# A two-layer decoder kernel: cross keys and values among the self scores, the cross norm with gamma and residual in two operations, the first pairs earlier, the performer reordered

## The chip, the cores and the metric

The kernel runs on one core of a Trainium2 chip. The metric is device microseconds (us) of one execution. The engines are TensorE (PE; its weight loads are PEld), VectorE (DVE), ScalarE (ACT), GpSimd (POOL) and SyncE (SP), which issues the transfers. Each runs its own list of instructions in order, and they wait for each other on semaphores.

## The reference

Six layers on x of 4 batches x 512 tokens x 256 channels, each followed by a residual and a layer norm:

```python
x = _layernorm(x + _L0_attn_ref(x, Wk, Wq, Wv))                      # causal softmax attention, 1 head
x = _layernorm(x + _L0_xattn_ref(x, ctx, ctx, mask, ...))            # cross attention, ends in:
    #   normed = (context - mu) * rsqrt(var + EPS);  return normed * ln_gamma + ln_beta
x = _layernorm(x + _L0_ffn_ref(x, k0, k1, k2, s0, s1, s2))           # three layers with weights +1 / -1
x = _layernorm(x + _L1_attn_ref(x, Wqkv, bqkv, Wout, bout, proj))    # performer, 16 heads of 16:
    #   q' = relu(q proj), k' = relu(k proj), 64 features a head, causal:
    #   out = sum_{s<=t} (q'_t . k'_s) v_s / (sum_{s<=t} q'_t . k'_s + 1e-6)
x = _layernorm(x + _L1_xattn_ref(x, ctx, ctx, ...))                  # mLSTM, 8 heads of 32, gates from x and ctx
x = _layernorm(x + _L1_ffn_ref(x, w1, conv_w, conv_b, w2))           # quantized layer, convolution, SiLU, quantized layer
```

## The kernel before

**Stages.** The work of a batch is cut in two. The front half has self attention (`self.`), cross attention (`cross.`), the sign layers (`sign.a`, `b`, `c`) and the performer (`perf.`). The back half has the mLSTM (`mlstm.`) and the quantized layers (`quant.`). The front half of batch b+1 is issued among the back half of batch b, so the program is: one front half alone, with the preparation of weights (`prep.`) in it, three middle stages with both, and one back half alone.

**Order.** Nothing is scheduled at run time. Each engine has a generator for each half, which yields a step's name (`cross.score0`) ahead of the step's instructions. `weave` takes from the generators in the order of a rank per step and engine, read from tables (`FRONT_TIMES`, `BACK_TIMES`, `PREP_TIMES`: name, then the ranks for PE, DVE, ACT, POOL), with `PERIOD` between batches and `LATER` between the halves. The order within a half's generator never changes by the ranks; how the two halves lie in each other does.

**Banks.** TensorE writes to 8 PSUM banks, 4 for each half, taken in rotation as the plan (`fb.use`, `bb.use`) lists them. A step that fills a bank waits until the bank's last user emptied it.

**Attention.** Scores of token tile i, the transposes ("turn") of tile i-1 and the products with the values of tile i-2 follow each other, i = 0 to 5. VectorE takes row maxima, ScalarE the exponential. The keys and values of the cross attention come from the context (`ctxT`) alone, so they depend on nothing that the self attention makes.

**Norms.** `stats` (DVE: statistics, aggregate, +eps), `rstd` (POOL: power), `normalize` (DVE: `shift`, tile 2p; ACT: tile 2p+1). Tiles go in pairs p = 0, 1; then TensorE turns a pair to channels (`xT0`, `xT1`), and DVE or ACT copy the result out of the bank. In the cross attention, the norm of the context is followed by DVE's product with gamma (L1434) and the residual (L1438), each of 256 columns per tile, and then by the statistics of the layer's own norm.

**Sign layers.** `sign.a` multiplies 8 column blocks m over 2 x 2 accumulated parts. The first four m are done for the first pair alone, while the second is still in its norm: L919 in the trace, then L928 for what is left, L938 for layer b, L948 for c.

**Performer.** Two chunks c of 8 heads. Projections: v (L803), q and k (L795); features of q and k (L974), keys' features turned (L983), the state (L1000) and its sums (L1530, L1532 on DVE); scores of two heads at a time (L1018), masked by DVE and ACT; then, for each group of four heads, the denominators (L1028) and the numerators (L1041), whose matmuls write to 32 rows of a bank with a column group of the array each:

```python
for i in range(2):
    for j in (2 * g, 2 * g + 1):
        ins = nc.tensor.matmul(num.bank[32 * j:32 * j + 32, here], ...
                               tile_position=(0, 32 * j), skip_group_check=True)
```

GpSimd sets `v_pad` and `p_sums` to zero in every batch, and copies the values into `v_pad`. Both lie in a region that other steps use too.

## Time and profile before

| | |
|---|---|
| three runs | 1008.03, 1002.79, 1007.87 us, median 1007.87 |
| profiled execution | 1005.53 us, of which the span from first to last instruction 1004.3 |
| mean granted TensorE clock | 0.867 of full |
| busy: PE / DVE / ACT / POOL | 805.1 / 622.3 / 357.8 / 169.6 us |
| DMA | 25 GB/s over the span |

Busy times are sums over the span; what a change is worth depends on which engine's work ends last at its place. The span splits into 0 to 207 us (front half alone), 207 to 429, 429 to 651, 651 to 873 (middle stages) and 873 to 1004 (back half alone). In the timeline rows a bracket behind a group of instructions gives the engine's idle time before it and who released it; a group's mean duration overlaps with its neighbours, because matmuls are pipelined. "L803" is line 803 of the kernel before. In the changed kernel the same lines stand 14 to 50 lines further down.

### The profile page before, as it was taken

Reading aid. Unit: us, or ns where it says so; the run is one execution under the profiler, and the core shown is the slowest. Engines: PE = TensorE matmul, PEld = TensorE weight load, DVE = VectorE, ACT = ScalarE, POOL = GpSimd, SP = SyncE. Lnnn points to the kernel's source line nnn. Section 1 sums busy time; section 2 is a strip of 40 time slices with the busy share of each in tenths; the row PEclk is TensorE's granted clock in tenths of the full one; section 3 lists DMA queues with packets and bytes.
Section 4 is the critical chain, followed back from the end, with each engine's and each line's share of the span. In section 5 each row is a group of like instructions: output and inputs, shape, how many; then the busy total and the mean of one; then the engine's idle time right before and its main releaser. Section 6 shows DMA issues by size and latency. Waiting matters only on the chain.

```text
span 1004.3 us, 14662 instructions
## 1 busy us (share of the span) xinstructions
PE 805.1 (80%) x5789; PEld 566.0 (56%) x5832; DVE 622.3 (62%) x1535; ACT 357.8 (36%) x646; POOL 169.6 (17%) x250
## 2 busy tenths in 40 slices
PE   8859877788999877888999877898999877739124
PEld 5545546666774545756774655766764555628112
DVE  2867322247487666656586767556685768455786
ACT  3242111125532254235432345244432445143062
POOL 3210110012322110012322300013312300003300
PEclk9989978699879979899979979998979978967565
DMA  9210000010010000020010000010000000000000
GB/s 367 104 43 1 1 21 1 1 64 22 1 43 1 1 22 1 1 85 22 1 43 1 1 22 2 1 64 1 24 19 1 1 1 1 23 0 1 0 0 21
DMA packets 13507, 25.85 MB, mean 26 GB/s; under 512 B 768, under 2 KB 7040, under 8 KB 13184
## 3 DMA queue, kind: packets, MB, share of 16 engines
q1 hardware_dynamic: 13440, 24.92, 7.2%
q8 instruction: 46, 0.75, 0.3%
q14 instruction: 21, 0.17, 0.1%
HBM read 22.82 MB, written 2.10 MB: 25 GB/s over the span
## 4 chain that ended last, share of the span: by engine, by line
PE 61%; DVE 24%; issue 7%; ACT 6%; POOL 2%; DVEq 0%; POOLq 0%; ACTq 0%
PE bank L938 11%; PE bank L795 7%; PE bank L803 6%; PE bank L1018 4%; PE bank L843 3%; PE bank L826 2%; PE bank L974 2%; PE bank L1041 2%; PE bank L948 2%; PE bank L928 2%; DVE stats L1289 2%; PE bank L788 1%; DVE work L1816 1%; DVE work L1785 1%; PE bank L1250 1%
## 5 line engine op out<-in xcount | busy, mean ns | idle before, releaser
L2110 POOL TENSOR_TENSOR rstd<-rstd,minus_half 128x2 f32<-128x2 f32 x56 | 40.3, 719 | 510.1 <-DVE rstd L1295 510.1
L938 PE MATMUL bank<-work,f0w 128*128 128x512 f16 x512 | 111.2, 379 | 0.0
L938 PEld LDWEIGHTS bank<-work,f0w 128*128 128x128 f16 x512 | 50.1, 98 | 60.4
L1959 ACT ACTIVATE work<-bank 128x512 f16<-128x512 f32 x64 | 37.3, 597 | 95.3 <-PE bank L938 76.5
L1477 DVE SCALAR_TENSOR_TENSOR work<-bank,work 128x512 f16<-128x512 f32 x64 | 41.7, 685 | 29.9 <-ACT work L1959 29.9
L1018 PE MATMUL bank<-work 64*128 64x128 f32 x512 | 44.5, 323 | 15.0 <-DVE work L1532 11.0
L1552 DVE TENSOR_TENSOR work<-bank,upper 128x512 f32<-128x512 f32 x32 | 22.1, 690 | 50.7 <-PE bank L1018 50.7
L1992 ACT ACTIVATE work<-bank 128x512 f32<-128x512 f32 x32 | 19.0, 592 | 90.1 <-PE bank L1018 90.1
L843 PE MATMUL bank<-work 128*128 128x256 f32 x208 | 50.6, 389 | 0.0
L1639 DVE TENSOR_TENSOR work<-work 128x512 f32<-128x512 f32 x32 | 25.7, 830 | 38.3 <-ACT work L2036 38.0
L1000 PE MATMUL bank<-work 128*128 128x34 f32 x192 | 35.5, 360 | 10.1 <-DVE work L1518 10.1
L1018 PEld LDWEIGHTS bank<-work 64*128 64x128 f32 x512 | 37.6, 222 | 9.5 <-issue 9.5
L843 PEld LDWEIGHTS bank<-work 128*128 128x128 f32 x208 | 39.1, 196 | 4.7
L1000 PEld LDWEIGHTS bank<-work 128*128 128x128 f32 x192 | 34.6, 281 | 11.6 <-ACT work L1978 11.6
L1197 PEld LDWEIGHTS bank<-work 128*128 128x128 f32 x256 | 39.3, 242 | 1.0 <-issue 1.0
L1373 DVE TENSOR_REDUCE small<-bank 128x1 f32<-128x512 f32 (+3 forms) x32 | 18.8, 587 | 33.7 <-PE bank L827 28.1
L1197 PE MATMUL bank<-work 128*128 128x33 f32 x256 | 39.0, 315 | 0.8 <-DVE work L1639 0.8
L1289 DVE BATCH_NORM_STATS2 stats<-y 128x6 f32<-128x256 f32 x96 | 36.1, 414 | 5.8 <-ACT y L1938 5.7
L974 PE MATMUL bank<-work,perf_w 32*128 32x512 f32 x128 | 23.0, 790 | 20.0 <-ACT work L1982 14.9
L2185 POOL TENSOR_TENSOR small<-small,minus_half 128x8 f32<-128x8 f32 x16 | 27.2, 1702 | 64.5 <-DVE small L1700 64.5
L2150 POOL COPY work<-work 128x256 f32<-128x256 f32 x16 | 10.2, 667 | 149.4 <-PE bank L1041 147.7
L1876 ACT ACTIVATE work<-bank,small 128x512 f32<-128x512 f32 (+3 forms) x32 | 19.4, 606 | 42.9 <-DVE small L1373 42.8
(271 smaller groups left out, 1860.8 us busy)
## 6 DMA issues: line engine op xcount, KB each, us to landing
ctxT<-in_ctxT SPq DMA_DIRECT2D x8, 512.0 KB, 4.7
work<-in_mask SPq DMA_DIRECT2D x4, 1024.0 KB, 5.9
xT<-in_xT SPq DMA_DIRECT2D x4, 512.0 KB, 3.6
work<-in_w SPq DMA_DIRECT2D x1, 2048.0 KB, 18.6
ctx<-in_ctx SPq DMA_DIRECT2D x4, 512.0 KB, 3.8
out<-y SPq DMA_DIRECT2D x4, 512.0 KB, 3.0
perf_w<-in_perf_w SPq DMA_DIRECT2D x1, 1536.0 KB, 16.3
x<-in_x SPq DMA_DIRECT2D x2, 512.0 KB, 6.3
```

Of the source, the lines that this page charges most:

```text
L795: ins = nc.tensor.matmul(u.bank[:, :], weights[:, k, c0:c0 + P], src[:, k, :], start=(k == 0), stop=(k == NC - 1))
L803: ins = nc.tensor.matmul(u.bank[:, j * C:(j + 1) * C], src[:, k, t * P:(t + 1) * P], weights[:, k, c0:c0 + C], start=(k == 0), stop=(k == ...
L843: ins = nc.tensor.matmul(u.bank[:, 0:C], probT[:, t % 2, j * P:(j + 1) * P], v[:, j, :], start=(j == 0), stop=(j == n - 1))
L938: ins = nc.tensor.matmul(u.bank[:, :], f0w1[:, k, m * P:(m + 1) * P], h1[part][:, k, :], start=(k == 0 and part == 0), stop=(k == NF - 1 a ...
L974: nc.tensor.matmul(u.bank[:, :], proj[rows, c, j * P:(j + 1) * P], src[rows, c, :], start=True, stop=True, tile_position=(32 * j, 0)).then ...
L1000: ins = nc.tensor.matmul(u.bank[:, o:o + 2 * PV1], kfs[:, t - 1, j * P:(j + 1) * P], p_v1[:, t - 1, h:h + 2, :].rearrange("p a b -> p (a b ...
L1018: ins = nc.tensor.matmul(u.bank[:, here], kf[rows, j, here], qf[rows, j, here], start=(i == 0), stop=True, tile_position=(PM * i, 0), skip ...
L1197: ins = nc.tensor.matmul(u.bank[:, h * LV1:(h + 1) * LV1], cT[:, h, t * P:(t + 1) * P], l_v1[:, t, h, :], start=True, stop=True)
L1289: m = vec.mark(nc.vector.bn_stats(s.stats[:, t, :], src[:, t, :]))
L1477: low_part(what, m, dst, number + m, lambda o, x, hi: nc.vector.scalar_tensor_tensor(out=o, in0=x, scalar=0.0, in1=hi, op0=ALU.max, op1=AL ...
L1959: nc.scalar.activation(dst[0][:, m, :], u.bank[:, :], ACT.Relu).then_inc(high_made.sem, 1)
L2110: nc.gpsimd.tensor_tensor(s.rstd[:, two], s.rstd[:, two], minus_half[:, 0:2], ALU.pow).then_inc(s.rstd_made.sem, 1)
```

## The change

Six things, in the order of the diff.

- All rank tables, `PERIOD` and `LATER` are changed.
- The four projections for the cross keys and values are issued among the self attention's steps, one behind each of the first four (`AMONG`), with a buffer of its own for the values (`c_v`).
- The cross norm: right behind its statistics, (y - mean) * gamma in one DVE operation per tile; then, when GpSimd's power is there, times rstd plus x in a second. ScalarE has no part in it any more.
- The first pair of the sign layers is evicted ahead of the norm of the second pair on both engines; three column blocks (before: four) are then multiplied for the first pair alone, ahead of `sign.xT1`.
- The performer: on ScalarE the copy of `xT0` ahead of the second norm; on TensorE xT0, v0, xT1, q and k of chunk 0, v1, features of q, q of chunk 1, features of k, k of chunk 1. Heads are taken in the order `taken`, so that every group of four has its numerators in four column groups. `v_pad` and `p_sums` are buffers of their own, set to zero once.
- x is loaded behind the context and the cross weights.

```diff
+AMONG = ("ck0", "ck1", "cv0", "cv1")
...
-PERIOD, LATER = 4120, 50
+PERIOD, LATER = 4780, 25
...
+    v_pad = sb("v_pad", [P, NT, HALF, 2, PD])
+    p_sums = sb("p_sums", [P, NT - 1, PAIRS, 32])
...
+    taken = [0, 3, 4, 7, 2, 1, 6, 5]
...
                 if 1 <= i <= NT:
                     turn_t(i - 1)
+                if i < len(among):
+                    yield f"{name}.{AMONG[i]}"
+                    among[i]()
                 if i >= 2:
...
+            yield from attention("self", b, front.xT, a_v, lambda t: bar_later[:, :], True,
+                                 [lambda: second_keys(0), lambda: second_keys(1),
+                                  lambda: second_values(0), lambda: second_values(1)])
...
+            yield "sign.xT0"
+            wait_normed(front, b, 2, 0)
+            to_channels(fb["sign", b, "xT", 0], fx[b % 2], 0)
+            yield "sign.early"
...
+            for m in range(3):
...
+            yield "sign.xT1"
...
-                for m2 in range(4) if m == 0 else ():
...
+                    if c == 0:
+
+                        yield f"perf.{made}.1"
+                        project_T(fb["perf", b, 1, made], wqkvT, {"q": 0, "k": C}[made] + P, front.xT)
...
-                        for i in range(2):
-                            for j in (2 * g, 2 * g + 1):
-                                ins = nc.tensor.matmul(num.bank[32 * j:32 * j + 32, here],
-                                                       v_pad[:, t, 2 * j + i, :, :].rearrange("p a b -> p (a b)"),
-                                                       inner[:, (2 * j + i) % 4, here], start=False, stop=(i == 1),
-                                                       tile_position=(0, 32 * j), skip_group_check=True)
+                        for r in range(4 * g, 4 * g + 4):
+                            h, j = taken[r], taken[r] // 2
+                            ins = nc.tensor.matmul(num.bank[32 * j:32 * j + 32, here],
+                                                   v_pad[:, t, h, :, :].rearrange("p a b -> p (a b)"),
+                                                   inner[:, r % 4, here], start=False, stop=(g == 1),
+                                                   tile_position=(0, 32 * j), skip_group_check=True)
...
+            def spread_by_gamma(p):
+
+                yield f"cross.in_norm{p}"
+                for t in (2 * p, 2 * p + 1):
+                    spread[t] = vec.mark(nc.vector.scalar_tensor_tensor(
+                        out=front.y[:, t, :], in0=front.y[:, t, :], scalar=front.mv[:, t, 0:1], in1=gamma,
+                        op0=ALU.subtract, op1=ALU.mult))
+
             def add_residual(p):
                 yield f"cross.add{p}"
-                dve.wait_ge(*front.normed_v.at(b, front.place[1, p]))
-                dve.wait_ge(*front.normed_s.at(b, front.place[1, p]))
-                for t in (2 * p, 2 * p + 1):
-                    m = vec.mark(nc.vector.tensor_tensor(front.y[:, t, :], front.y[:, t, :], gamma, ALU.mult))
-                dve.wait_ge(*m)
+                dve.wait_ge(*front.rstd_made.at(b, front.place[1, p]))
+                dve.wait_ge(*spread[2 * p + 1])
                 dve.wait_ge(*front.shifted.at(b, NT - 1))
                 for t in (2 * p, 2 * p + 1):
-                    added[t] = vec.mark(nc.vector.tensor_tensor(front.y[:, t, :], front.y[:, t, :], fx[b % 2][:, t, :],
-                                                                ALU.add))
...
+                    added[t] = vec.mark(nc.vector.scalar_tensor_tensor(
+                        out=front.y[:, t, :], in0=front.y[:, t, :], scalar=front.rstd[:, t:t + 1], in1=fx[b % 2][:, t, :],
+                        op0=ALU.mult, op1=ALU.add))
...
+        nc.gpsimd.memset(v_pad[:, :, :, :, :], 0.0).then_inc(constants_by_gpsimd, 1)
+        nc.gpsimd.memset(p_sums[:, :, :, :], 0.0).then_inc(constants_by_gpsimd, 1)
...
-            pool.wait_ge(*v1_ones.at(b))
-            nc.gpsimd.memset(v_pad, 0.0)
-            nc.gpsimd.memset(p_sums, 0.0).then_inc(blocks_zeroed.sem, 1)
-            pool.wait_ge(*blocks_zeroed.at(b))
```

How the tables and the code together move instructions shows in the order of each engine.

TensorE at the start of the performer in a middle stage, before: `ident,x` are the pairs turned, `perf_w` the projections and the features (L974), `work,f1w` the quantized layer and `identb,work` the turns of the back half.

```order
L788 MATMUL bank<-ident,x 128x128 x4
L1204 MATMUL bank<-ident,small 128x128 x4
L803 MATMUL bank<-perf_w,xT 128x256 x4
L788 MATMUL bank<-ident,x 128x128 x4
L1216 MATMUL bank<-identb,work 128x128 x4
L795 MATMUL bank<-work,f1w 128x512 x12
L803 MATMUL bank<-perf_w,xT 128x256 x4
L795 MATMUL bank<-xT,perf_w 128x512 x8
L974 MATMUL bank<-work,perf_w 128x512 x8
L795 MATMUL bank<-work,f1w 128x512 x4
L983 MATMUL bank<-perf_w,work 128x128 x12
L1000 MATMUL bank<-work 128x34 x12
```

And with the change (L1002 are the features; L809 with `xT,perf_w` x2 are q and k of one chunk):

```order
L802 MATMUL bank<-ident,x_other 128x128 x4
L809 MATMUL bank<-xT,perf_w 128x512 x4
L817 MATMUL bank<-perf_w,xT 128x256 x4
L1002 MATMUL bank<-work,perf_w 128x512 x4
L809 MATMUL bank<-xT,perf_w 128x512 x2
L1002 MATMUL bank<-work,perf_w 128x512 x4
L809 MATMUL bank<-xT,perf_w 128x512 x2
L1015 MATMUL bank<-perf_w,work 128x128 x12
L809 MATMUL bank<-work,f1w 128x512 x4
L1032 MATMUL bank<-work 128x34 x12
L809 MATMUL bank<-work,f1w 128x512 x2
L1044 MATMUL bank<-bar_upper,identb 128x512
```

The values of the first pair stand ahead of the turning of the second, chunk 1's q and k between and behind the features, and six matmuls of the back half next to the state (L1032, before L1000).

VectorE in the first front half, between the last row maximum of the cross attention and its residual, before (L1434 and L1438 are gamma and residual):

```order
L1289 BN_STATS stats<-y 128x6 x2
L1292 BN_AGGR mv<-stats 128x2 x2
L1295 TENSOR_SCALAR rstd<-mv 128x2
L1377 RECIPROCAL small<-small 128x1
L1301 SCALAR_TENSOR_TENSOR shift<-mv,rstd 128x2
L1304 TENSOR_SCALAR y<-y,mv,rstd 128x256
L1434 TENSOR_TENSOR y<-y,rows_all 128x256 x2
L1438 TENSOR_TENSOR y<-y,x 128x256 x2
L1289 BN_STATS stats<-y 128x6 x2
```

And with the change (L1467 is the spread by gamma; L1364 and L1366 turn a block of weight bits to +1 and -1, and six such pairs stand ahead of these rows, behind L1467):

```order
L1364 TENSOR_SCALAR f0w<-ctxT 128x1024
L1366 TENSOR_SCALAR f0w<-f0w,s_cols 128x1024
L1369 TENSOR_SCALAR f0w<-y 128x512 x4
L1477 SCALAR_TENSOR_TENSOR y<-y,rstd,x 128x256 x2
L1321 BN_STATS stats<-y 128x6 x2
L1324 BN_AGGR mv<-stats 128x2 x2
L1327 TENSOR_SCALAR rstd<-mv 128x2
L1321 BN_STATS stats<-y 128x6 x2
L1324 BN_AGGR mv<-stats 128x2 x2
```

The preparation of the sign weights, which stood among the steps of the self attention, stands between spread and residual (L1477).

TensorE at the cross attention in a middle stage, before: L1122 are the back half's gate scores, `ident,x` and L895 the turned pairs and their queries, L826 and L827 the cross scores, L1138 to L1150 the columns of the mLSTM's gates.

```order
L834 MATMUL bank<-ident,work 128x128 x4
L843 MATMUL bank<-work 128x256 x7
L795 MATMUL bank<-ctxT,cross_w 128x512 x4
L803 MATMUL bank<-cross_w,ctxT 128x256 x8
L1122 MATMUL bank<-xT,ctxT 128x128 x16
L788 MATMUL bank<-ident,x 128x128 x4
L895 MATMUL bank<-xT,cross_w 128x256 x4
L788 MATMUL bank<-ident,x 128x128 x4
L895 MATMUL bank<-xT,cross_w 128x256 x4
L826 MATMUL bank<-work 128x512 x2
L827 MATMUL bank<-work,identb 128x512
L1138 MATMUL bank<-small,ones 128x72
```

And with the change (L1154 are the gate scores, L802 and L915 the pairs and queries, L840 the scores, L848 and L857 turns and products):

```order
L848 MATMUL bank<-ident,work 128x128 x4
L857 MATMUL bank<-work 128x256 x7
L1154 MATMUL bank<-xT,ctxT 128x128 x32
L802 MATMUL bank<-ident,x 128x128 x4
L915 MATMUL bank<-xT,cross_w 128x256 x4
L802 MATMUL bank<-ident,x 128x128 x4
L915 MATMUL bank<-xT,cross_w 128x256 x4
L840 MATMUL bank<-work 128x512 x2
L841 MATMUL bank<-work,identb 128x512
L840 MATMUL bank<-work 128x512 x2
L841 MATMUL bank<-work,identb 128x512
L848 MATMUL bank<-ident,work 128x128 x4
```

Both lots of gate scores stand together, the projections of keys and values (L795, L803 with `cross_w`) have gone ahead among the self scores, and the columns stand behind the cross attention's products.

## Rows read from the trace of the kernel before

**Rows 1.** The page's part 4: the chain of waits by engine and by line.

```profile
PE 61%; DVE 24%; issue 7%; ACT 6%; POOL 2%; DVEq 0%; POOLq 0%; ACTq 0%
PE bank L938 11%; PE bank L795 7%; PE bank L803 6%; PE bank L1018 4%; PE bank L843 3%; PE bank L826 2%; PE bank L974 2%; PE bank L1041 2%; PE bank L948 2%; PE bank L928 2%; DVE stats L1289 2%; PE bank L788 1%; DVE work L1816 1%; DVE work L1785 1%; PE bank L1250 1%
```

**Rows 2.** Windows by stage: window, its length, busy us (instructions) by engine, granted clock, DMA.

```profile
429.00:651.00 222.00, 193.55 (x1445) 137.00 (x1455) 148.10 (x366) 87.44 (x157) 40.71 (x58) 0.92 0.06 20
585.00:601.00 16.00, 13.05 (x123) 9.96 (x117) 12.79 (x26) 8.39 (x14) 0.00 (x0) 0.61 0.01 2
118.00:158.00 40.00, 29.08 (x161) 19.94 (x162) 10.96 (x27) 6.82 (x13) 5.87 (x10) 0.70 0.05 14
```

**Rows 3.** Timeline of PE: one lot of denominators (L1028) and of numerators (L1041).

```profile
603.49 0.64 PE L1028 MATMUL bank<-work,head_col 128*32 128x128 f32 x16 [0.20 <-DVE work L1552]
603.95 1.92 PE L1041 MATMUL bank<-work 128*32 128x128 f32 x32
```

**Rows 4.** Groups by line and shape, weight loads, 429 to 651 us.

```profile
L1041 PEld LDWEIGHTS bank<-work 128*32 128x32 f32 x128 | 7.0, 110 | 0.0
L1028 PEld LDWEIGHTS bank<-work,head_col 128*32 128x32 f32 x128 | 3.0, 109 | 3.0 <-DVE work L1552 2.5
```

**Rows 5.** Timeline of PE, performer in a middle stage.

```profile
565.59 1.99 PE L803 MATMUL bank<-perf_w,xT 128*128 128x256 f32 x8 [1.74 <-ACT xT L1850]
...
581.29 1.14 PE L974 MATMUL bank<-work,perf_w 32*128 32x512 f32 x8 [0.94 <-DVE work L1507]
584.25 2.09 PE L974 MATMUL bank<-work,perf_w 32*128 32x512 f32 x8 [1.81 <-ACT work L1982]
...
590.22 4.48 PE L1000 MATMUL bank<-work 128*128 128x34 f32 x24 [1.34 <-DVE work L1518]
595.98 2.08 PE L1018 MATMUL bank<-work 64*128 64x128 f32 x16 [1.28 <-DVE work L1532]
...
623.61 3.81 PE L1000 MATMUL bank<-work 128*128 128x34 f32 x24 [1.20 <-DVE work L1518]
```

**Rows 6.** Timeline of PE: the performer's state in the first front half.

```profile
147.67 5.30 PE L1000 MATMUL bank<-work 128*128 128x34 f32 x24 [1.31 <-DVE work L1518]
```

**Rows 7.** Timeline of PE, cross attention to second sign layer (L938), middle stage.

```profile
468.62 1.97 PE L895 MATMUL bank<-xT,cross_w 128*128 128x256 f32 x8 [0.87 <-DVE xT L1281]
470.42 1.88 PE L826 MATMUL bank<-work 128*128 128x512 f32 x4
474.24 0.41 PE L1138 MATMUL bank<-small,ones 8*128 8x72 f32 x2 [1.94 <-DVE small L1632]
...
526.16 4.05 PE L938 MATMUL bank<-work,f0w 128*128 128x512 f16 x18
```

**Rows 8.** Groups by line and shape, ACT, 429 to 651 us: copies of gate scores.

```profile
L2013 ACT ACTIVATE work<-bank 128x512 f32<-128x512 f32 x8 | 4.1, 597 | 0.0
```

**Rows 9.** Timeline of PE, first front half: pairs turned for the sign layers.

```profile
67.82 0.63 PE L788 MATMUL bank<-ident,x 128*128 128x128 f32 x4 [4.00 <-DVE x L1304]
...
73.12 1.08 PE L788 MATMUL bank<-ident,x 128*128 128x128 f32 x4 [4.56 <-ACT x L1857]
```

**Rows 10.** Groups by line, DVE, 28 to 60 us: preparing the sign weights.

```profile
L1334 DVE TENSOR_SCALAR f0w<-f0w,s_cols 128x1024 f16<-128x1024 f16 x8 | 4.2, 530 | 0.3
L1332 DVE TENSOR_SCALAR f0w<-xT 128x1024 f16<-128x1024 uint8 x4 | 3.8, 947 | 0.0
L1332 DVE TENSOR_SCALAR f0w<-ctxT 128x1024 f16<-128x1024 uint8 x4 | 2.7, 686 | 0.0
```

**Rows 11.** The chain of waits, first front half, cross norm: start, us, what.

```profile
67.97 0.61 ACT y L1857
...
68.67 0.77 DVE y L1434 x2
```

**Rows 12.** Timeline of DVE around the last front half's end.

```profile
872.29 0.74 DVE L1289 BATCH_NORM_STATS2 stats<-y 128x6 f32<-128x256 f32 x2
...
878.83 0.16 DVE L1301 SCALAR_TENSOR_TENSOR shift<-mv,rstd 128x2 f32<-128x2 f32 x1 [0.81 <-POOL rstd L2110]
```

787 lines of the change are left out of this document (402 added, 385 removed).

## The prediction

> **What bounds the kernel now.** First the chain of waits, which says whose work sets the end: TensorE 61% of it, VectorE 24%, and no transfer among the leading lines [rows 1]. The program is a pipeline: the front half of batch b+1 runs beside the back half of batch b. The windows by stage show one middle stage of 222.0 us with TensorE busy for 193.55, VectorE for 148.10, at a granted clock of 0.92 [rows 2]. Three such stages (207 to 873), the first front half alone (0 to 207) and the last back half alone (873 to 1004) make the span of 1004.3 us. So time comes out of a middle stage in three ways: TensorE's 28 us without work, work that it does at a low clock, and work that gets shorter. Then the timeline of TensorE, read where the gaps are. They lie where one tensor is handed from engine to engine: in the start of the performer [rows 5], in the cross attention and the norm behind it [rows 7], and, in the first front half, where no back half fills them, in both [rows 6, 9]. Behind such gaps the clock is low: 0.61 from 585 to 601, 0.70 from 118 to 158 [rows 2].
>
> The sum is made against the profiled execution: 1005.53 us, that is the span and 1.2 us around it. The median of the runs is 2.3 us above it.
>
> **The change, part by part.**
>
> Performer numerators. 32 matmuls fall in every group of four heads: two groups, two chunks, four batches, so 16 such lots, all on the chain (L1041 is 2% of it [rows 1]). Now neighbours use two column groups in turn and take 1.92 us. The denominators beside them, 16 matmuls of the same shape over four column groups, take 0.64 us [rows 3]. The reordered heads put four column groups into each lot, so 32 should take 2 x 0.64 = 1.28: 0.64 less by these rows, 0.45 less against the 1.73 us that the lot holds the chain. I take 0.56, times 16: **-9 us**. Bounds: nothing, if it is the loading of a new weight for every matmul that sets the pace (128 loads keep the loader busy for 7.0 us here, for 3.0 in the denominators, at the same 110 and 109 ns each [rows 4]); or half of 1.92, -15.
> The Trainium skill ("TensorEngine Tiling (Array Packing)", Key Properties) says that tiles work independently and load and multiply in parallel; four groups for two would then halve the lot, -15 us by the rule against -9 by the row. No row here shows these loads over four groups.
>
> Performer start, middle stages. The same matmuls are ordered anew, so what counts is the gaps [rows 5]. At 565.59 TensorE waited 1.74 us for ScalarE's copy of xT; that copy now stands ahead of the second norm on ScalarE: about 0.6 less. At 581.29, 0.94 for the eviction of the last keys; now values stand between: gone. At 584.25, 1.81 for the first features; now q of chunk 1, four matmuls of 512 columns, stands between: gone. At 590.22, 1.34, and at 595.98, 1.28, on VectorE; lots of 4 and 2 matmuls of the back half's quantized layer now stand there, which stood elsewhere: 0.9 and 0.4 less. Sum 4.65. I take **-4 us** a stage, three times -12: a little is lost because the chain's VectorE work (with SiLU and convolution work of the back half between) does not get shorter. Bounds: 0, if VectorE is what is late and the gaps only move to the state; -7.5, if with the gaps the low clock goes too (the state at 590.22 takes 4.48 us, at 623.61, at a higher clock, 3.81).
>
> Performer start, first front half. The same gaps, with no back half to fill them, and all the work of 124 to 158 at half clock: the state takes 5.30 us [rows 6] for 3.81, and the features 2.09 for 1.14, as at 584.25 and 581.29 [rows 5]. The two gaps that fall, as long as those at 581.29 and 584.25, give 2.7; the clock, if it stays up, another 5 to 6 over the stretch. I take **-7 us**, bounds -3 and -10.
>
> Cross attention in the middle stages. Keys and values now stand among the self scores. TensorE had work there anyway, so nothing is removed. What moves: the back half's gate scores (L1122, 2 x 16 matmuls, one lot each side of the projections) now stand next to each other. The second lot needs banks that ScalarE has to empty, four copies of 0.597 us [rows 8]: a wait of some 2 us. On VectorE the gate's sum g, its row maximum and the negative of it now stand ahead of the copy of the second xT, some 2 us more in all: the query projection, 0.87 late today [rows 7], is 2 to 3 late. So the first cross score comes some 4 us later than at 470.42 [rows 7]. Behind it the reverse: the columns' matmuls at 474.24 waited 1.94 us for VectorE's columns, now they come after the four cross score lots. The norm with gamma loses a ScalarE pass and VectorE's gamma products (0.61 and 0.77 us [rows 11]) and the shift ahead of them; the product by gamma now lies beside GpSimd's power. Each of two chains is 1.5 to 1.7 us shorter. And the first pairs are turned before the second norm, so that early matmuls cover its latency. From first score to the second sign layer it is 55.7 us today [rows 7]; I estimate 50.7. Net **-1 us** a stage, -3 in all, and either sign is open: bounds -5 and +13 (below).
>
> First front half, cross norm. VectorE's preparation of the sign weights was spread over 30 to 55 us, beside TensorE's self attention. Now seven pairs of operations, three of 0.95 + 0.53 us and four of 0.69 + 0.53 [rows 10], and four small ones, an estimated 9.9 to 10.7 us together, stand in one lump between the spread by gamma and the residual. TensorE has only the last cross products beside it. The pairs that it waits for at 67.82 and 73.12 [rows 9] would come at about 73 and 77; the shorter norm gives 1.7 twice, the early matmuls some more. I take **+3 us**, bounds 0 and +7.
>
> Last stage. The evictions of the performer's output on VectorE stood behind one norm of the back half: its statistics start at 872.29 [rows 12]. That norm is 0.74 for the statistics, some 0.4 for their aggregation, 0.81 of waiting for GpSimd [rows 12] and some 0.6 for shift and scale: 2.5 us. Now two norms and a residual product of some 0.5 stand ahead, 5.6 us. Less the slack at the second projection, **+2.5 us** where nothing covers it; in a middle stage front work of the next batch does, +0.5, which is inside the -4 and -1. Bounds 0 and +3.5.
>
> The zeroing of two buffers once instead of per batch is on GpSimd, behind the constants at the start, and saves work later on an engine that is busy for 41 of 222 us [rows 2]: nothing. The changed order of the loads: nothing, no transfer stands on the chain [rows 1]; if the later load of x is late, it is by less than one load, and only once.
>
> Sum: -9 - 12 - 7 - 3 + 3 + 2.5 = -25.5, 1005.5 - 25.5 = **980 us**.
>
> **The rivals.**
> *It goes nowhere.* VectorE and GpSimd chains, not TensorE's order, are late: the performer's gain (-19) is only -6, the numerators give -4, the cross attention loses 2 a stage, the lump 6. Then -6 - 4 + 6 + 6 + 2.5: 1005 to 1008. For it: the waits at 590.22 and 595.98 name VectorE [rows 5]. Against: those at 565.59 and 584.25 name ScalarE, which is free. 0.11.
> *Slower.* The place is TensorE ahead of the first cross score. Two waits of 2 to 3 us each, close together, are what is seen ahead of low clocks: a gap of 4.00 and one of 4.56 at 67.82 and 73.12 [rows 9], the short gaps of rows 5 ahead of 0.61. If the clock falls there, the cross attention (an estimated 12 to 13 us at full speed: four lots of scores of 1.88 [rows 7], products and turns of two thirds of that) takes twice as long: with the waits, +13 a stage less what the norm gives back, some +10; three times 30, less the 25.5 + 3 of the rest: +2 at least, and with the lump at its bound and little from the performer +12, so 1007 to 1018. It decides from 9 us a stage. Against: today's gaps of 0.87 and 1.94 [rows 7] lie in the same place, and the stage still has a clock of 0.92. 0.15.
> *The numerators don't speed up*, all else as forecast: 985 to 995. The equal load times of rows 4 speak for it, the row of denominators, which also load each time, against. 0.12.
> *More.* The clock stays up in all performer starts and in the norm: middle stages at -12: 957 to 965. 0.10.
>
> **How the numbers follow.** The forecast (966 to 994) has 0.52. Slower and nowhere together have 0.26, so the range ends at 1007, where about 0.12 is left above; below 957 some 0.08 is left. What a measurement of this kernel can tell from no change is about 0.5%, 5 us. Faster: 0.52 + 0.12 + 0.10 = 0.74; same 0.11; slower 0.15.
>
> **What would show it.** In the changed kernel's timeline: numerator lots of 1.2 to 1.4 us; performer start without waits on the features, first performer scores 4 us earlier against the end of the sign layers (8 in the first front half), and a clock above 0.8 where it was 0.61; a lump of VectorE preparation beside an idle TensorE near 65 to 75 us; middle stages of 214 to 216 us. A wait of over 2 us ahead of the first cross score, with half clock behind it, would make the prediction wrong towards slower; numerator lots still at 1.9 would take 9 us from it.

## The result, and the profile after

The changed kernel takes 976.79 us in the median of four runs (971.01 to 992.32), the kernel before 1005.33 (1002.71 to 1008.03) beside it: the ratio is 0.970, 95% interval 0.961 to 0.978. The forecast was 980, in a range of 957 to 1007. Ratios leave out runs more than 1.5% above the fastest of their kernel; medians are over all runs.

The changed kernel spreads over 20 us, the kernel before over 5. Six more runs of it (experiment c1 below) had their median at 984.96; over all ten it is 982. Where experiments are compared with it, a difference of medians under some 8 us therefore says little by itself, and the stretches of one profiled execution decide. Its own profiled execution took 971.75 us, near its fast end.

The page of the changed kernel, parts 1, 2 and 4: busy time, granted clock in 40 slices, and the chain. Its span is 970.5 us.

```profile
PE 771.9 (80%) x5816; PEld 524.1 (54%) x5816; DVE 615.4 (63%) x1519; ACT 354.0 (36%) x638; POOL 165.3 (17%) x244
...
PEclk9978998798899999899899998999899997857565
...
PE 63%; DVE 26%; ACT 5%; issue 4%; POOL 1%; DVEq 0%; ACTq 0%
```

TensorE is busy for 33.2 us less, and the span is 33.8 us shorter; its share of the chain is 63%, 61% before [rows 1]. The mean granted clock rises from 0.867 to 0.899. TensorE's time without work is the same over the whole span, 199.2 us before and 198.6 after: what fell is its busy time. Windows of a middle stage, of the performer's start in it, and of the performer's start in the first front half, which answer to [rows 2]:

```profile
412.00:624.00 212.00, 183.63 (x1452) 125.25 (x1453) 146.97 (x363) 86.55 (x155) 39.67 (x56) 0.97 0.07 21
554.00:570.00 16.00, 11.25 (x74) 5.71 (x73) 9.61 (x15) 9.42 (x18) 1.83 (x3) 1.00 0.11 34
118.00:150.00 32.00, 24.31 (x154) 15.31 (x153) 12.45 (x35) 6.69 (x12) 5.13 (x9) 0.94 0.06 17
```

TensorE's time without work in the stage has hardly moved: 28.4 us now, 28.45 before. What fell is its busy time, by 9.9 us, and with it the low clock: 0.61 has become 1.00, and 0.70 has become 0.94.

The table shows where the 33.8 us lie, read from the starts of matmuls on TensorE. A stage runs from the start of the performer's output product in one batch to that of the next; the last column is the back half alone.

| us | first front half | middle 1 | middle 2 | middle 3 | last back half |
|---|---|---|---|---|---|
| before | 206.7 | 222.0 | 221.9 | 221.9 | 131.9 |
| changed | 198.0 | 213.8 | 211.6 | 213.6 | 133.5 |
| difference | -8.7 | -8.2 | -10.3 | -8.3 | +1.6 |

The second middle stage by stretch. The last column adds up TensorE's waits in the stretch (the brackets of its timeline), before and after:

| us | before | changed | difference | forecast | waits |
|---|---|---|---|---|---|
| output product to first cross score | 41.7 | 44.0 | +2.3 | +4 | 3.7, 6.0 |
| first cross score to second sign layer (L938, now L961) | 55.7 | 48.6 | -7.2 | -5 | 4.1, 1.6 |
| second sign layer to third | 27.6 | 27.6 | 0 | 0 | 0, 0 |
| third sign layer to first performer score | 42.2 | 40.5 | -1.7 | -4 | 9.3, 9.1 |
| first performer score to output product | 54.6 | 51.0 | -3.6 | -2.2 (4 lots) | 11.0, 11.7 |

PE's timeline, one lot of denominators and numerators, and the weight loads of the same lines over the stage, for [rows 3, 4]:

```profile
578.75 0.64 PE L1060 MATMUL bank<-work,head_col 128*32 128x128 f32 x16 [0.20 <-DVE work L1602]
579.22 1.06 PE L1073 MATMUL bank<-work,v_pad 128*32 128x128 f32 x32
...
612.44 1.08 PE L1060 MATMUL bank<-work,head_col 128*32 128x128 f32 x32
```

```profile
L1073 PEld LDWEIGHTS bank<-work,v_pad 128*32 128x32 f32 x128 | 3.6, 110 | 0.0
L1060 PEld LDWEIGHTS bank<-work,head_col 128*32 128x32 f32 x128 | 3.1, 109 | 2.0 <-DVE work L1602 1.4 <-issue 0.2
```

A lot takes 1.06 us where it took 1.92. One load still takes 110 ns, but the loader is busy for 3.6 us instead of 7.0. The 128 loads add up to 14.1 us, so in the mean two lay over each other before and four do now: loads of different column groups overlap. Over the whole span the loader's time for these lots falls from 28.1 to 14.3 us and the matmuls' from 30.7 to 16.9, by the same 13.8.

PE's timeline at the performer's start in a middle stage, for [rows 5], and the first two waits and the state in the first front half, for [rows 6]:

```profile
541.84 1.99 PE L817 MATMUL bank<-perf_w,xT 128*128 128x256 f32 x8 [0.67 <-ACT xT L1900]
...
556.84 1.14 PE L1002 MATMUL bank<-work,perf_w 32*128 32x512 f32 x8 [1.33 <-DVE work L1540]
558.62 1.98 PE L809 MATMUL bank<-xT,perf_w 128*128 128x512 f32 x4 [0.64 <-ACT work L2035]
561.47 1.14 PE L1002 MATMUL bank<-work,perf_w 32*128 32x512 f32 x8 [0.87 <-ACT work L2018]
563.25 1.98 PE L809 MATMUL bank<-xT,perf_w 128*128 128x512 f32 x4 [0.64 <-ACT work L2035]
566.17 0.95 PE L1015 MATMUL bank<-perf_w,work 32*128 32x128 f32 x24 [0.94 <-DVE work L1548]
...
568.43 2.84 PE L1032 MATMUL bank<-work 128*128 128x34 f32 x24 [0.34 <-DVE work L1566]
...
572.16 0.39 PE L1044 MATMUL bank<-bar_upper,identb 128*128 128x512 bf16 x1 [0.46 <-DVE work L1583]
```

```profile
122.35 1.97 PE L817 MATMUL bank<-perf_w,xT 128*128 128x256 f32 x8 [0.72 <-issue]
...
143.79 2.88 PE L1032 MATMUL bank<-work 128*128 128x34 f32 x24 [1.30 <-DVE work L1566]
```

The waits are not gone. They are cut into pieces of 0.34 to 1.33 us, with matmuls of some 2 us between, and from the third sign layer to the first score they add up to 9.1 us, 9.3 before. In the first front half they do shrink, from 10.9 to 7.7 us, 2.6 of it at the copy of `xT0` (0.72 for 3.33). The state now takes 2.84 us where it took 4.48 and 5.30: it does the same work at the full clock.

PE's timeline at the cross attention of a middle stage, for [rows 7]:

```profile
447.92 1.17 PE L1154 MATMUL bank<-xT,ctxT 32*128 32x128 f32 x32 [2.23 <-ACT work L2069]
...
450.35 1.99 PE L915 MATMUL bank<-xT,cross_w 128*128 128x256 f32 x8 [0.68 <-ACT xT L1900]
...
454.04 1.97 PE L915 MATMUL bank<-xT,cross_w 128*128 128x256 f32 x8 [1.25 <-DVE xT L1313]
455.84 1.88 PE L840 MATMUL bank<-work 128*128 128x512 f32 x4
...
504.40 1.89 PE L961 MATMUL bank<-work,f0w 128*128 128x512 f16 x8
```

The wait of 2.23 us on ScalarE's copies of gate scores stands where the forecast put one of some 2, and the query projection is 1.25 late. In this stage and the third no low clock follows. In the first middle stage one does, behind the same wait of 2.23 us: the granted clock is 0.51 from 235 to 242 us, and the query projection takes twice as long:

```profile
236.94 3.78 PE L915 MATMUL bank<-xT,cross_w 128*128 128x256 f32 x8 [0.68 <-ACT xT L1900]
```

There the first cross score comes 4.5 us later than before, not 2.3. Behind the first score, to the second sign layer, it is 48.56 us, 55.74 before, in all three middle stages. 2.6 us of that are waits; most of the rest is the clock ahead of the second sign layer, 0.53 from 509 to 520 before, 1.00 from 486 to 505 now.

The first front half, DVE's lump (its first pair and the residual behind it; six more pairs like the first and four small operations lie between) and PE beside it, for [rows 9, 10]:

```profile
58.38 0.68 DVE L1364 TENSOR_SCALAR f0w<-xT 128x1024 f16<-128x1024 uint8 x1
59.09 0.48 DVE L1366 TENSOR_SCALAR f0w<-f0w,s_cols 128x1024 f16<-128x1024 f16 x1
...
67.58 0.87 DVE L1477 SCALAR_TENSOR_TENSOR y<-y,rstd,x 128x256 f32<-128x256 f32 x2
```

```profile
62.08 3.78 PE L857 MATMUL bank<-work 128*128 128x256 f32 x8 [3.76 <-ACT work L1948]
72.32 1.09 PE L802 MATMUL bank<-ident,x 128*128 128x128 f32 x4 [6.46 <-DVE x L1336]
```

The wait of 3.76 us is not VectorE's. ScalarE sums the sizes of the quantized layer's weights (L1917) from 56.56 to 61.47 us, 4.9 us in one piece, and the copy that TensorE waits for (L1948) stands behind it.

The last place is the end of the last front half, where the quantized layer's norm releases the pair for the mLSTM:

```profile
837.01 3.72 PE L817 MATMUL bank<-perf_w,y 128*128 128x256 f32 x16 [1.40 <-DVE y L1616]
846.93 1.09 PE L802 MATMUL bank<-ident,x 128*128 128x128 f32 x4 [6.20 <-ACT x L1907]
```

### The profile page after: what moved, and what is told of

It is laid out like the page before. It is cut to its first block, busy times and chain, and to the rows that moved or that the text cites. A ratio compares the mean times of both kernels' runs of the same rounds, so it can differ in the third digit from the quotient of the medians.

```text
span 970.5 us, 14621 instructions
## 1 busy us (share of the span) xinstructions
PE 771.9 (80%) x5816; PEld 524.1 (54%) x5816; DVE 615.4 (63%) x1519; ACT 354.0 (36%) x638; POOL 165.3 (17%) x244
## 4 chain that ended last, share of the span: by engine, by line
PE 63%; DVE 26%; ACT 5%; issue 4%; POOL 1%; DVEq 0%; ACTq 0%
PE bank L961 11%; PE bank L809 5%; PE bank L817 5%; PE bank L840 4%; PE bank L857 3%; PE bank L1050 3%; PE bank L1229 2%; PE bank L951 2%; PE bank L1032 2%; DVE work L1819 2%; PE bank L1002 2%; PE bank L971 2%; DVE work L1825 2%; PE bank L802 2%; DVE work L1828 1%
## 5 line engine op out<-in xcount | busy, mean ns | idle before, releaser
L961 PE MATMUL bank<-work,f0w 128*128 128x512 f16 x512 | 111.3, 379 | 0.0
L961 PEld LDWEIGHTS bank<-work,f0w 128*128 128x128 f16 x512 | 50.1, 98 | 60.2
L857 PE MATMUL bank<-work 128*128 128x256 f32 x208 | 51.6, 391 | 3.8 <-ACT work L1948 3.8
L1405 DVE TENSOR_REDUCE small<-bank 128x1 f32<-128x512 f32 (+3 forms) x32 | 18.9, 590 | 54.6 <-PE bank L841 54.5
L1689 DVE TENSOR_TENSOR work<-work 128x512 f32<-128x512 f32 x32 | 27.3, 860 | 27.4 <-ACT work L2092 27.2
L857 PEld LDWEIGHTS bank<-work 128*128 128x128 f32 x208 | 39.0, 195 | 9.1 <-ACT work L1948 4.2
L1050 PE MATMUL bank<-work 64*128 64x128 f32 x512 | 41.8, 309 | 0.0
L1050 PEld LDWEIGHTS bank<-work 64*128 64x128 f32 x512 | 35.1, 209 | 8.6 <-issue 8.6
L809 PE MATMUL bank<-xT,perf_w 128*128 128x512 f32 x64 | 30.7, 612 | 8.2 <-ACT work L2035 5.1
L1229 PE MATMUL bank<-work 128*128 128x33 f32 x256 | 33.4, 288 | 0.8 <-DVE work L1689 0.8
L1229 PEld LDWEIGHTS bank<-work 128*128 128x128 f32 x256 | 33.2, 209 | 1.5 <-issue 1.5
L1032 PE MATMUL bank<-work 128*128 128x34 f32 x192 | 28.2, 313 | 7.1 <-DVE work L1566 7.1
L1570 DVE TENSOR_SCALAR work<-bank 128x512 f32<-128x512 f32 x24 | 15.8, 688 | 27.5 <-PE bank L1002 27.1
L1032 PEld LDWEIGHTS bank<-work 128*128 128x128 f32 x192 | 27.4, 230 | 9.4 <-ACT work L2031 9.4
```

Source lines behind the costliest of these rows:

```text
L809: ins = nc.tensor.matmul(u.bank[:, :], weights[:, k, c0:c0 + P], src[:, k, :], start=(k == 0), stop=(k == NC - 1))
L857: ins = nc.tensor.matmul(u.bank[:, 0:C], probT[:, t % 2, j * P:(j + 1) * P], v[:, j, :], start=(j == 0), stop=(j == n - 1))
L961: ins = nc.tensor.matmul(u.bank[:, :], f0w1[:, k, m * P:(m + 1) * P], h1[part][:, k, :], start=(k == 0 and part == 0), stop=(k == NF - 1 a ...
L1032: ins = nc.tensor.matmul(u.bank[:, o:o + 2 * PV1], kfs[:, t - 1, j * P:(j + 1) * P], p_v1[:, t - 1, h:h + 2, :].rearrange("p a b -> p (a b ...
L1050: ins = nc.tensor.matmul(u.bank[:, here], kf[rows, pair, here], qf[rows, pair, here], start=(i == 0), stop=True, tile_position=(PM * i, 0) ...
L1229: ins = nc.tensor.matmul(u.bank[:, h * LV1:(h + 1) * LV1], cT[:, h, t * P:(t + 1) * P], l_v1[:, t, h, :], start=True, stop=True)
```

## The experiments

Twelve kernels ran: ten with one edit to the changed kernel, one without an edit (c1), and one that joins two (d1). Each figure is a median with its range and number of runs, then the ratio to the kernel before on the same chip.

**a1, two column groups again.** The heads in their natural order, the matmuls of a lot alternating between two groups. All else stays changed.

```diff
-    taken = [0, 3, 4, 7, 2, 1, 6, 5]
+    taken = list(range(8))
...
-                        for r in range(4 * g, 4 * g + 4):
+                        for r in (4 * g, 4 * g + 2, 4 * g + 1, 4 * g + 3):
...
-                                                   inner[:, r % 4, here], start=False, stop=(g == 1),
+                                                   inner[:, r % 4, here], start=False, stop=(h % 2 == 1),
```

> The changed kernel with the heads in their natural order and the numerators' matmuls taking two column groups in turn, as before the change; all else as changed. Theory (the lots of numerators got shorter because neighbouring matmuls now stand in four column groups): each of the 16 lots goes back from 1.06 us to about 1.92, the performer's second part of every stage grows by 4 x 0.86 = 3.4 us, and the whole by 13 to 14 us against 971.8, so about 985. Rival (the shorter lots come from the new buffer of the padded values or from a clock that is higher there): lots stay near 1.1 us and the time within 3 us of the changed kernel.

Measured: 993.87 us (987.62 to 1002.39, 4), ratio 0.9895 (0.983 to 0.996). Its lot:

```profile
156.10 1.92 PE L1073 MATMUL bank<-work,v_pad 128*32 128x128 f32 x32
```

The lot is back at 1.92. 16 x 0.86 = 13.8 us of the difference to the changed kernel are the lots, which TensorE shows as 30.7 us busy against 16.9 over 512 matmuls. The rest, 3 us by medians, is inside the spread. `v_pad` is a buffer of its own here too, so the new buffer does not shorten the lots.

**b5, two groups, in pairs one behind the other.** Does the taking turns matter, or the number of groups?

```diff
-    taken = [0, 3, 4, 7, 2, 1, 6, 5]
+    taken = list(range(8))
...
-                                                   inner[:, r % 4, here], start=False, stop=(g == 1),
+                                                   inner[:, r % 4, here], start=False, stop=(h % 2 == 1),
```

> The changed kernel with the heads in their natural order and the numerators' matmuls in that order too, so that two neighbours stand in one column group before the next follows (groups 0 0 1 1). Theory (a matmul in a column group waits for the one ahead of it in the same group, and different groups run beside each other): the lot of 32 takes longer than the 1.92 us of groups in turn, 2.5 us or more, and the kernel is 5 us or more slower than with two groups in turn (987.6 at the least). Rival (only how many groups a lot touches counts): 1.92 us again.

Measured: 991.39 us (989.61 to 995.98, 4), ratio 0.988 (0.985 to 0.991).

```profile
590.34 1.94 PE L1073 MATMUL bank<-work,v_pad 128*32 128x128 f32 x32
```

Groups 0 0 1 1 take 1.94 us, groups 0 1 0 1 take 1.92, four groups 1.06. The number of groups in a lot counts; the order of two groups does not.

**a2, the copy behind the norm.** In the first batch ScalarE copies `xT0` behind the second norm, as before.

```diff
-            yield "perf.xT0"
-            copy_pair(fb["perf", b, "xT", 0], front.xT, 0)
+            if b > 0:
+                yield "perf.xT0"
+                copy_pair(fb["perf", b, "xT", 0], front.xT, 0)
             yield from normalize(front, b, 3, front.y, fx[b % 2], 1, "sign.")
+            if b == 0:
+                copy_pair(fb["perf", b, "xT", 0], front.xT, 0)
```

> The changed kernel with ScalarE's copy of the performer's first turned pair behind the second pair's norm again, in the first front half alone. Theory (this copy was the 3.33 us gap ahead of the first values, and the gap was what lowered the clock behind it): the gap ahead of the first values grows from 0.72 to about 3.3 us, and the performer's first part runs at half clock: from the last sign layer to the first performer score 6 to 9 us more, the whole 6 to 9 us more, about 979. Rival (the clock is set by the many short gaps behind, not by this one): only the 2.6 us of the gap, about 974 to 975.

Measured: 982.86 us (979.63 to 993.06, 4), ratio 0.981 (0.974 to 0.988).

```profile
124.81 2.85 PE L817 MATMUL bank<-perf_w,xT 128*128 128x256 f32 x8 [3.33 <-issue]
```

The gap of 3.33 us is back for 0.72, and the projection behind it takes 2.85 for 1.97. From the third sign layer to the first performer score the first front half takes 37.8 us instead of 34.0, 2.5 of it waits, and as a whole 201.4 instead of 198.0. So this copy is 3.8 of the 9 us that the performer's start gained there. The low clock of the whole stretch did not come back with it: the state takes 3.07 us.

**a3, chunk 1's q and k ahead of the features.** The order of before on TensorE and on the engines that evict; nothing else.

```diff
             yield from values(1)
+            for made in "qk":
+                yield f"perf.{made}.1"
+                project_T(fb["perf", b, 1, made], wqkvT, {"q": 0, "k": C}[made] + P, front.xT)
             for c in range(NC):
...
-                    if c == 0:
-
-                        yield f"perf.{made}.1"
-                        project_T(fb["perf", b, 1, made], wqkvT, {"q": 0, "k": C}[made] + P, front.xT)
...
```

> The changed kernel with the queries and keys of chunk 1 projected ahead of the features again, in all batches. Theory of the prediction (they cover TensorE's waits at the features): 2 to 3 us more in each of four performer starts, 8 to 12 us in all, 980 to 984. Theory from the trace after the change (with four banks in rotation every lot waits for an eviction of the lot before, 0.64 and 0.87 us, wherever the projections stand, so the waits were only cut up): between -2 and +3 us in all, 970 to 975.

Measured: 989.98 us (989.24 to 997.49, 4), ratio 0.987 (0.982 to 0.991). The lot of projections now lies in one piece, and the old waits behind it are back:

```profile
353.80 1.14 PE L1003 MATMUL bank<-work,perf_w 32*128 32x512 f32 x8 [0.93 <-DVE work L1545]
356.76 1.14 PE L1003 MATMUL bank<-work,perf_w 32*128 32x512 f32 x8 [1.81 <-ACT work L2033]
359.37 0.95 PE L1012 MATMUL bank<-perf_w,work 32*128 32x128 f32 x24 [1.47 <-DVE work L1569]
```

From values to first score the middle stages take 30.2, 34.3 and 31.7 us, against 30.7, 30.7 and 30.6. In the first of them the order alone costs nothing. In the second and third the same instructions take 3.6 and 1.0 us longer. TensorE's waits from the third sign layer to the first score are 8.2 to 8.6 us here and 9.1 in the changed kernel, so the reordering removes no waiting. In the middle stages it keeps the clock up. All four runs have a mean clock of 0.866 to 0.870, as low as before the change, where the changed kernel's ten have 0.879 to 0.903. And the state, which comes right behind, takes 3.00, 5.17 and 3.24 us in this kernel's middle stages, 4.48 or 4.49 in the kernel before, and 2.84 to 2.95 in all thirty middle stages of the ten profiled executions that have the new order and no filling matmuls. What that is worth is not shown: none of the four runs came under 989 us, but other stretches, which the edit leaves alone, were longer in this execution too.

**a4, the preparation spread.** The ranks of the weight preparation go back among the steps of the self and cross attention, VectorE's and also ScalarE's sums of sizes (`prep.abs`).

```diff
-    ("prep.w00", None, 445, None, None),
+    ("prep.w00", None, 230, None, None),
...
-    ("prep.w11", None, 520, None, None),
-    ("prep.w12", None, 520, None, None),
+    ("prep.w11", None, 380, None, None),
+    ("prep.w12", None, 424, None, None),
...
-    ("prep.abs00", None, None, 516, None),
+    ("prep.abs00", None, None, 370, None),
...
```

> The changed kernel with the preparation of the sign weights on VectorE and of the sums of sizes on ScalarE put into the gaps of the self and cross attention of the first front half; three of the twelve VectorE steps stay between the spread by gamma and the residual. Theory (the lump of 9.2 us on VectorE between 58.4 and 67.6, and 4.9 us on ScalarE from 56.6 to 61.4, make the first pair late): the first pair is turned at 65 to 67 instead of 72.3, the second sign layer begins 5 to 7 us earlier, the whole falls by 4 to 7 us, to 965 to 968. Rival (the gap of 3.76 us before the last product and the norm's own chain hold it): less than 2 us earlier.

Measured: 969.29 us (968.88 to 976.98, 4), ratio 0.966 (0.962 to 0.971).

```profile
55.34 3.62 PE L857 MATMUL bank<-work 128*128 128x256 f32 x16
65.63 1.09 PE L802 MATMUL bank<-ident,x 128*128 128x128 f32 x4 [6.67 <-DVE x L1336]
```

The gap of 3.76 us inside the products is gone, the one ahead of the pair is not: it is the latency of two norms. From first cross score to the first sign matmul it is 27.2 us instead of 33.4. The two lumps, VectorE's and ScalarE's, cost 6.2 us there; they were not spread one at a time. The first front half as a whole is only 1.6 us shorter, 196.5 against 198.0: the next stretch takes 1.2 more, and from the third sign layer to the first performer score, and from there to the output product, it is 2.3 and 1.6 more, with the same instructions and the same waits (7.7 and 11.6 us), so by the clock.

**b1, keys and values behind the self attention.**

```diff
-        plan_attention("self", b, [("cross", b, "k", 0), ("cross", b, "k", 1), ("cross", b, "v", 0), ("cross", b, "v", 1)])
+        plan_attention("self", b)
...
-    ("self.cv0", 147, 180, None, None),
+    ("self.cv0", 147, 216, None, None),
...
```

> The changed kernel with the cross keys' and values' projections behind the self attention again, on all engines; all else as changed. Theory (TensorE had work there anyway; in the first front half the stretch from the self queries to the first cross score is 32.4 us in both kernels): 0 to 1.5 us a stage, the time within 5 us of the changed kernel's 971 to 977. Rival (they fill the softmax's waits in the self attention, which the changed rank tables count on): 3 us or more in every stage, 984 and up.

Measured: 1006.99 us (998.83 to 1037.75, 10), ratio 1.000 (0.997 to 1.004): the whole gain is gone. The profiled execution was the longest of the ten, so its lengths are not used, only what waits:

```profile
465.90 1.09 PE L851 MATMUL bank<-ident,work 128*128 128x128 f32 x4 [3.53 <-ACT work L1931]
...
481.42 1.17 PE L1159 MATMUL bank<-xT,ctxT 32*128 32x128 f32 x32 [2.23 <-ACT work L2074]
```

With the projections away, the last turns of the self attention wait 3.53 us for ScalarE's exponential. The wait on the gate scores is the same 2.23. So in the changed kernel, with its rank tables, the projections among the scores fill waits. They are not what the change gained: the kernel before has them behind too, and its waits from the output product to the first cross score are 3.7 us a stage, where they are 9.4 here and 5.6 to 6.0 in the changed kernel. The loss is not the clock alone either: two runs with a mean clock of 0.890 take 999.34 and 998.83 us, two of the changed kernel with 0.891 take 981.83 and 982.08. The other half's steps lie otherwise in the changed tables, and the projections belong to them.

**b2, the gate scores apart.** The second lot behind the queries, by its rank.

```diff
-    ("mlstm.raw1", 238, None, 397, None),
+    ("mlstm.raw1", 275, None, 397, None),
```

> The changed kernel with the second lot of the back half's gate scores moved on TensorE from ahead of the cross attention's pairs to behind its first score, by one rank. Theory (the wait of 2.23 us that the prediction foresaw, for ScalarE's four copies, is a loss): it goes, the first cross score of each middle stage comes 3.3 us earlier and the first sign layer 2 us earlier; 3 x 2.2 = 6 to 7 us less in all, 964 to 970. Rival (the pair's norm on VectorE, which the copy of the second turned pair waits behind, holds the queries anyway): the wait moves to the pairs, less than 2 us in all.

Measured: 988.34 us (986.09 to 1003.64, 4), ratio 0.983 (0.979 to 0.987).

```profile
664.74 1.17 PE L1154 MATMUL bank<-xT,ctxT 32*128 32x128 f32 x32
668.58 0.63 PE L802 MATMUL bank<-ident,x_other 128*128 128x128 f32 x4 [2.66 <-issue]
```

The 2.23 us are not saved. They stand ahead of the turned pair now, 2.66 us. The releaser is not named, but ScalarE's list shows it: the four copies of gate scores (2.06 us from 665.93) stand ahead of its tile of the pair's norm (0.62 us from 667.86), so TensorE waits for ScalarE's copies in both kernels, only at another step. Another order on ScalarE was not tried.

**b3, gamma behind the power.** VectorE waits for GpSimd's power before it multiplies by gamma.

```diff
                 yield f"cross.in_norm{p}"
+                dve.wait_ge(*front.rstd_made.at(b, front.place[1, p]))
```

> The changed kernel with the product by gamma made to wait for GpSimd's power, so that it no longer lies beside it. Theory (the overlap is part of the chain's gain): 0.8 us for each of two pairs in the first front half, where nothing covers it, and 0 to 0.8 for the second pair in a middle stage: 1.5 to 4 us in all. Rival (VectorE has other work in that time anyway, preparation in the first front half and the mLSTM's later): nothing, within 1 us in the stages' lengths.

Measured: 998.83 us (990.39 to 1005.56, 10), ratio 0.993 (0.990 to 0.996). VectorE and GpSimd in the middle stage:

```profile
488.16 0.17 DVE L1327 TENSOR_SCALAR rstd<-mv 128x2 f32<-128x2 f32 x1
496.95 0.88 DVE L1468 SCALAR_TENSOR_TENSOR y<-y,mv,rows_all 128x256 f32<-128x256 f32 x2 [8.62 <-POOL rstd L2169]
```

```profile
490.04 3.48 POOL L2227 TENSOR_TENSOR work<-ctx,small 128x256 f32<-128x256 f32 x6 [13.43 <-ACT small L2086]
493.49 2.77 POOL L2173 TENSOR_TENSOR x<-x,rows_all 128x256 f32<-128x256 f32 x4
496.21 0.71 POOL L2169 TENSOR_TENSOR rstd<-rstd,minus_half 128x2 f32<-128x2 f32 x1
```

The power was asked for at 488.3 and made at 496.9: ten operations of the back half stand ahead of it in GpSimd's list. In the changed kernel the same queue lets the power start at 480.02, 10 us after VectorE's request at 469.96, but the product with gamma does not hang on it. In the kernel before, GpSimd had been idle for 12.85 us when the power was asked for. So the product beside the power is worth more than the 0.81 us of [rows 12]: with it behind, VectorE stands still for 8.62 us, and the back half's work in its list with it. The stretch from score to first sign matmul is 38.7 to 39.2 us in the middle stages for 36.9, and 35.3 for 33.4 in the first. Those 1.8 to 2.4 us at four places make 8 of the 27 us by which the profiled execution is longer than the changed kernel's (the medians are 22 apart, where 4 at most were expected). Most of the rest lies in stretches that the edit leaves alone.

**b4, the last norms spread.** Performer evictions on VectorE between the quantized layer's two norms, by rank.

```diff
-    ("perf.spread.1", 1886, 1522, 1812, None),
+    ("perf.spread.1", 1886, 1560, 1812, None),
...
-    ("quant.norm0", None, 1592, 1925, None),
+    ("quant.norm0", None, 1520, 1925, None),
```

> The changed kernel with the last layer's two norms on VectorE moved ahead of and between the performer's last masks, away from the place ahead of the performer's output. Theory (the two norms and a residual product ahead of the copies cost 2.5 us where the last back half stands alone, and 0.5 in the middle stages): the last stage falls by 2 to 3 us, the others by 0 to 1: 968 for 971. Rival (they then delay the masks, for which TensorE waits): the last performer part grows by as much.

Measured: 993.44 us (990.63 to 996.74, 4), ratio 0.988 (0.984 to 0.993).

```profile
856.05 5.41 PE L817 MATMUL bank<-perf_w,y 128*128 128x256 f32 x16 [1.40 <-DVE y L1616]
865.20 0.63 PE L802 MATMUL bank<-ident,x 128*128 128x128 f32 x4 [3.73 <-ACT x L1907]
```

The gap is back at 3.73 us from 6.20, yet the last back half takes 133.5 us in both: the output product ahead of it ran at a lower clock, 5.41 us for 3.72. The same execution holds a comparison of another kind, two middle stages with the same instructions:

```profile
198.00:412.00 214.00, 185.83 (x1450) 126.84 (x1450) 146.87 (x361) 84.70 (x154) 39.56 (x56) 0.95 0.06 18
412.00:634.00 222.00, 193.23 (x1450) 132.39 (x1450) 146.52 (x362) 86.29 (x156) 40.17 (x56) 0.92 0.06 20
```

8 us between two stages of one program, at a clock of 0.95 and 0.92, with VectorE busy for the same time (146.87 and 146.52 us). That is as much as a whole stage gained by the change. A third of it, 2.7 us, lies between first cross score and second sign layer, and there the order of events can be read. The mLSTM's product (L1229) in the second of the two stages, and in the first:

```profile
489.68 2.27 PE L1229 MATMUL bank<-work 128*128 128x33 f32 x16 [1.99 <-DVE work L1689]
```

```profile
275.02 1.94 PE L1229 MATMUL bank<-work 128*128 128x33 f32 x16 [0.15 <-DVE work L1689]
```

In the faster stage the columns ahead of this product run at a low clock (0.66 from 256 to 266 us), TensorE arrives when VectorE is ready, and the clock behind is 1.00 (272 to 293). In the slower stage the columns run at the full clock (1.00 from 472 to 482), TensorE is early, waits 1.99 us, and the clock behind the wait is 0.76 (486 to 507). Up to the product the slower stage had gained 3.3 us; from there to the second sign layer it loses 6.0, 1.8 by the wait and the rest by the clock. Time gained ahead of a place where VectorE is late comes back as a wait, and the wait is followed by the low clock.

**c1, the changed kernel again**, six runs beside c2, without an edit.

> The changed kernel once more, unaltered, with more runs and another profile, as the level for the other experiments. Theory (its short waits lie where the granted clock falls in some executions and not in others): the runs spread over some 20 us, 970 to 992, while the kernel before stays within 6; where the profile is longer than 970.5, the surplus stands in stages with half-clock rows and not in other waits, in steps of 2 to 11 us a stage. Rival (the other experiments are slow of themselves): all runs within 5 us of 972.

Measured: 984.96 us (970.91 to 991.83, 6), ratio 0.970 (0.965 to 0.975). The spread came as expected, and the rival, all runs within 5 us, fell. The profiled execution was one of the longer ones, 987.84 us at a clock of 0.884; its middle stages take 220.4, 218.3 and 216.4 us. From the third sign layer to the first performer score they take the same 40.5 us as in the changed kernel's first profile; the surplus lies behind the first cross score (51.3 to 51.5 for 48.6) and in the performer's second part (52.9 to 54.8 for 51.0 to 52.9).

**c2, the short waits filled.** Matmuls whose result nothing reads are put ahead of TensorE's waits, into the bank that the waiting step fills next: 8 at the gate scores, 3 or 4 at the queries, 6 at the first sign layer, 3 at each hand-over of the performer.

```diff
+        def fill(u, n):
+            pe.wait_ge(*u.free)
+            for _ in range(n):
+                nc.tensor.matmul(u.bank[:, :], identb[:, :], bar_upper[:, :, :].rearrange("p a b -> p (a b)"),
+                                 start=True, stop=True, skip_group_check=True)
...
+                    fill(four[0], 3)
                     for u in four:
...
```

> The changed kernel with matmuls that compute nothing (identity by a constant, into a bank that the next step owns and overwrites) put on TensorE ahead of its waits: 8 between the lots of gate scores, 3 or 4 ahead of the queries, 6 ahead of the first sign matmuls, 3 at each hand-over of the performer, some 60 a batch. Nothing that is computed changes. Theory (a large part of the change's gain, and its spread, is the clock, which falls behind short waits): the granted clock rises from 0.90 to 0.93 or more, every middle stage is at or below 211.6 us, half-clock rows at the mLSTM's columns and at the performer's second state go, 955 to 968 with a spread below 6 us. Rival (the waits as such cost the time and the clock follows the amount of real work): no stage below 211, and the added matmuls that do not fit into a wait add 0.1 to 0.4 us each place, 980 or more.

Measured: 974.78 us (969.83 to 975.41, 6), ratio 0.969 (0.966 to 0.972), mean clock 0.913 in the profiled execution. Its timeline at the gate scores (L828 is the filling):

```profile
443.52 1.67 PE L828 MATMUL bank<-bar_upper,identb 128*128 128x512 bf16 x7 [0.16 <-issue]
445.59 1.17 PE L1167 MATMUL bank<-xT,ctxT 32*128 32x128 f32 x32 [0.39 <-ACT work L2084]
```

Against c1 the median is 10 us lower and all six runs lie within 5.6 us, where c1's lie within 21; their mean clocks are 0.911 to 0.915, where c1's are 0.879 to 0.903. The ratios are the same, 0.969 and 0.970. So filling raises the clock and steadies the kernel, but it does not beat the best runs, and of what was expected (955 to 968 us, a clock of 0.93, no middle stage over 211.6) only the spread came. The middle stages take 213.5, 215.1 and 215.2 us, longer than in the changed kernel's profile. The later two lose 3.4 us between first cross score and second sign layer, by what b4 showed: the clock at the columns is full (1.00 from 466 to 480), TensorE waits 1.99 us for VectorE ahead of the mLSTM's product, and the clock behind is 0.68 (480 to 496).

**d1, filled and spread.** a4's ranks, and c2 with fewer filling matmuls where nothing waited long.

```diff
-    ("prep.w11", None, 520, None, None),
+    ("prep.w11", None, 380, None, None),
...
+                fill(u, 0 if m else 4)
...
```

> The two edits that helped, together: the preparation of the sign weights spread, and the waits filled, with fewer filling matmuls where they had delayed real ones (4 for 6 ahead of the first sign matmuls, none ahead of the cross pairs, of the second sign pair and of the performer's first pair, 2 for 3 ahead of the first values, 1 for 3 ahead of the state). Theory: the first front half at 191 to 193 us (spread alone 196.5 with the clock down behind it, filled alone 196.1), middle stages at 211 to 213.5, in all 962 to 968, and all runs within 6 us. Rival (the fillings cost what they give): 969 or more, no better than spreading alone.

Measured: 966.35 us (959.05 to 969.47, 6), ratio 0.9605 (0.957 to 0.964): the fastest version here. The window of its first front half:

```profile
0.00:190.00 190.00, 164.48 (x1161) 102.89 (x1161) 91.25 (x233) 51.29 (x105) 24.91 (x41) 0.95 0.19 71
```

The first front half takes 190.2 us instead of 198.0, the middle stages 210.8 to 213.7, as in the changed kernel's profiled execution (211.6 to 213.8). c2 alone has a first front half of 196.1 us, so with the waits filled the spread preparation is worth 5.9 us to its end, where it was 1.6 without: most of a4's 6.2 us arrive. That the filled waits are what keeps them is the likely reading; d1 also has fewer fillings than c2.

## Why the prediction was right, and where it was not

The sign and the size held: 25.5 us were forecast against 28.5 by the medians and 33.8 in the two profiled executions. Of the mechanism, the numerators held. What did not hold is that the rest would come from waits that go: TensorE's waits are the same in sum, and the time came from shorter lots and a higher clock. The size is in part luck, in two ways. In the profiled executions the performer starts of the middle stages gave 5.4 us for 12, while the cross attention gave 12.5 for 3 and the numerators 13.8 for 9. And single runs lie between 970.9 and 992.3 us.

Two of the rivals' sums were added up wrong as well: "goes nowhere" makes +4.5 by its own terms, 1010 us and not 1005 to 1008, and "slower" sets 30 against 28.5, although without the cross attention's -3 the rest is 22.5, which makes some 1013. Term by term:

**Numerators, -9 forecast, -13.8 measured.** The term was mis-sized. The row of denominators gave 1.28 for a lot, the lot takes 1.06. The step was the doubling: 16 denominators take 0.64 us and 32 of them in one piece, at 612.44, take 1.08, so 0.2 us of a row comes once, however long it is. The rule of the Trainium skill ("TensorEngine Tiling (Array Packing)", Key Properties), that tiles load and multiply independently, was weighed and put at -15; by the 3.6 us of loader time for 7.0 and a lot of 0.55 times the old one, the trace agrees with it nearly in full. The doubt drawn from [rows 4] was that every matmul loads a new weight of 110 ns: it still does, beside others. The denominators' row in [rows 4] had said so already, with 128 such loads over four groups in 3.0 us. The loads may set the pace, since loader and matmuls fell by the same 13.8 us, and yet the lot is shorter. b5 shows that it is the number of groups, not their order. The rival "numerators don't speed up" fell.

**Performer start in the middle stages, -4 a stage forecast, -1.7 to -1.9 measured.** The step that failed is "now values stand between: gone" and the same for q of chunk 1. The wait for `xT0` shrank as forecast (1.74 to 0.67). Of the waits at the features, 0.94 and 1.81 became 1.33, 0.64, 0.87, 0.64 and 0.94. Four banks go round between projections and features, so an interposed projection needs a bank that an eviction has to empty, and the next wait is behind it: by the releasers, the projections wait 0.64 us for the eviction of features (L2035), and the features 0.87 for that of the projection (L2018). The sum of the waits is 9.1 us for 9.3, so all of the 1.7 us is work at a higher clock; the state alone gave 1.6. a3 shows the order to gain nothing where the clock stays (30.2 us against 30.7). What came with the cut waits is the clock, 1.00 for 0.61 here and 0.94 for 0.70 in the first front half, and with a3 part of it goes again; which of the waits brought it down before was not varied alone.

**Performer start, first front half, -7 forecast, -9.0 measured** (43.0 to 34.0 us from layer c to first score). The waits fell by 3.2 us, not at the features, as forecast, but at the copy of `xT0`, to which a2 gives 3.8 in all. The other 5.8 are the clock, inside the 5 to 6 that the forecast named, with the state at 2.88 for 5.30. (Before, not all the work of the stretch ran at half clock: the projections of q and k took 7.13 us for 16, and the first features 1.14, as at full clock.) Some 2 of the 5.8 hang on the execution: a4, b1, b2 and b5 have the same order and waits of 7.7 us, and take 36.1 to 36.5 with a state of 4.97 to 5.30.

**Cross attention, -1 a stage forecast, -4.9 in two stages and -2.7 in the first.** Both halves went the right way: the first cross score comes 2.3 us later (4.5 in the first middle stage) against 4, and the stretch behind is 7.2 shorter against 5. Two terms were mis-sized. The query projection was to be 2 to 3 us late and is 1.25 late, beside the 2.23 at the gate scores. And behind the first score the forecast counted only shorter chains: the waits gave 2.6 us, and the other 4.6 came from the clock, chiefly at the mLSTM's product and the first sign matmuls, for which no term stood. b1 shows that the changed tables need the projections among the scores, not that this place gained against the kernel before. And b3 shows that gamma ahead of the power lets VectorE go on during a GpSimd queue of 8 to 10 us, which the change itself brought: the cross attention is earlier now, and its norm meets the back half's work on GpSimd. The forecast knew only the 0.81 us of [rows 12].

**Cross norm of the first front half, +3 forecast, +1.4 measured** (43.3 to 44.7 us from first cross score to second sign layer; another 1.2 us are lost in the program's first 9 us, for which no term stood). The lump lies where it was put and lasts 9.2 us, against 9.9 to 10.7. Beside it lies one on ScalarE of 4.9 us that the forecast did not name, and TensorE's wait of 3.76 us is on that. Without both, a4, the stretch is 39.7 us, 3.6 below the kernel before. So the shorter norm and the early pairs gave 3.6 where they were reckoned at 3.4 and some more, and the two lumps cost 5.

**Last stage, +2.5 forecast, +1.6 measured**, with the wait ahead of the pair at 6.20 for 3.73. b4 brings the wait back to 3.73 and gains nothing: the clock was lower ahead of it.

**What no term held: the clock in the middle stages.** Part of the gain is work that did not change and takes less time. Of 33.2 us less of TensorE's busy time, 13.8 are the numerators; the state (35.5 to 28.2 us), the features (23.0 to 18.2) and the mLSTM's L1229, before L1197 (39.0 to 33.4), make 17.7 more, with equal counts of the same shapes. If TensorE was always at one of its two levels, 1.2 and 2.4 GHz, a mean of 0.867 over 1004.3 us is 267 us at the lower one, and 0.899 over 970.5 is 196. The rival "slower" was this same mechanism with the opposite sign: a wait of 2.23 us came where it had one, and in one of three middle stages the low clock followed, for 2.2 us and not for the 10 it put on every stage. The rival "more" was nearer to the truth in the middle stages (-8 to -10 against its -12).

Left open: why the same wait of 2.23 us is followed by the low clock in one stage and not in another, and so why the kernel runs in 971 or in 992 us. Filled waits narrow it (c2), so the short waits have a part in it; the runs don't show what starts a fall. Nor was it tried to let the power go ahead of the ten mLSTM operations on GpSimd.

## What to carry to other kernels

Add up the waits of a stretch before and after, and do not only follow one gap. A wait that is only moved or cut up is worth little by itself, but several short ones in place of a long one can keep the clock up, and work that ran at a higher clock made about half of the gain here; so compare what unchanged work costs behind each gap before and after. Where the next engine is late, time gained ahead can come back as a wait, here with a low clock behind it. Matmuls of 32 columns should be laid out so that neighbours use four column groups rather than two. When work is interposed to cover a wait, count the banks in rotation: the cover needs one too, and waits for its own eviction.

## What was not expected of the hardware

- 32 matmuls over four column groups take 1.06 us, over two 1.92 in turn and 1.94 in pairs. A load takes 109 or 110 ns in all cases, and the loader is busy for 14.3 us over four groups and 28.1 and 28.4 over two, for 512 loads.
- The changed program's time varies by 21 us from run to run (970.9 to 992.3) where the kernel before varies by 7 (1001.6 to 1008.3, beside all experiments), and it follows the mean granted clock: 0.903 in the shortest runs, 0.879 in the longest.
- A stage whose columns run at a low clock is shorter than one where they run at the full clock (b4, 48.6 for 51.3 us in the stretch), because of a wait of 1.99 us and the low clock behind it.
- Matmuls without use in the waits took the spread to 5.6 us (969.8 to 975.4), while the shortest run stayed at 970.
